# Gated linear attention beside a mixture of experts: exponentials one step later, and two waits among GpSimd's transfers

## What is computed

```python
xn = _layernorm(x, axis=-1)
x = x + _L0_attn_ref(xn, ...) + _L0_ffn_ref(xn, ...)

# attention, with gc the running sum of the log gates inside a chunk
A = jnp.einsum('bhntd,bhnsd->bhnts', q, k)
A = A * jnp.where(mask, jnp.exp(jnp.where(mask, dec, 0.0)), 0.0)   # dec = gc[t] - gc[s]
o_intra = jnp.einsum('bhnts,bhnsd->bhntd', A, v)
...
on = o * jax.lax.rsqrt(jnp.mean(o * o, axis=-1, keepdims=True) + EPS) * gnorm_w
o = on * (g * jax.nn.sigmoid(g))
return o @ Wo

# experts
for e in range(NUM_EXPERTS):
    h = jax.nn.gelu(x_flat @ w1[e] + b1[e], approximate=False)
    y = h @ w2[e] + b2[e]
    sel = expert_idx == e
    out = out + jnp.where(sel, expert_w, 0.0)[:, None] * y
```

## Time and profile before

| | us |
|---|---|
| median of 3 runs | 411.32 |
| lowest, highest | 410.52, 411.75 |
| the profiled execution | 410.52 |
| its span, first to last instruction | 408.6 |
| TensorE busy | 386.7 (95%) |
| VectorE busy | 326.3 (80%) |
| ScalarE busy | 304.5 (75%) |
| GpSimd busy | 276.6 (68%) |

### The profile page before, as it was taken

One profiled execution on the slowest core, in us unless ns is written; L12 is line 12 of the kernel. 1 busy time (PEld: TensorE's weight loads), 2 busy tenths in 40 slices (PEclk: granted clock), 3 DMA queues, 4 the chain that ended last, 5 costly groups with the idle time before them and its releaser, 6 DMA issues.

```text
span 408.6 us, 13495 instructions
## 1 busy us (share of the span) xinstructions
PE 386.7 (95%) x3650; PEld 337.1 (83%) x3651; DVE 326.3 (80%) x868; ACT 304.5 (75%) x947; POOL 276.6 (68%) x237
## 2 busy tenths in 40 slices
PE   7988899999999999999999999899999999999990
PEld 6656788877788888888888878799999999999990
DVE  5989898999988898889888888667687687687750
ACT  4889998787887978797888887466666676666660
POOL 6012534268888888888888833178888888888884
PEclk9999999999999999999999999999999999999996
DMA  8846586464555445474655340145545555455530
GB/s 237 230 158 193 177 288 245 120 186 129 170 179 162 128 127 168 143 200 140 186 155 154 115 137 14 44 63 69 69 68 65 66 69 67 63 67 71 64 32 0
DMA packets 59096, 51.29 MB, mean 126 GB/s; under 512 B 7200, under 2 KB 51392, under 8 KB 59072
## 3 DMA queue, kind: packets, MB, share of 16 engines
q1 hardware_dynamic: 45936, 42.07, 36.0%
q0 software_dynamic: 12272, 8.54, 15.1%
q10 hardware_dynamic: 864, 0.40, 0.4%
HBM read 33.14 MB, written 18.30 MB: 126 GB/s over the span
## 4 chain that ended last, share of the span: by engine, by line
PE 80%; DVE 6%; ACT 4%; DMA 3%; issue 3%; POOL 2%; SPq 1%; ACTq 0%; DVEq 0%; POOLq 0%
PE psA L912 16%; PE psVG L900 16%; PE psVG L721 9%; PE psO L756 8%; PE psA L737 7%; PE psT L790 6%; PE psQK L709 6%; PE psT L782 4%; PE psKS L747 3%; PE psO L770 3%; ACT E L1080 2%; SPq L343 1%; DMA x_all<-in_L_attn_x_dram 1%; DMA gcB<-decay_rows 1%; PE psQK L891 1%
## 5 line engine op out<-in xcount | busy, mean ns | idle before, releaser
L579 POOL DMA_INDIRECT out_dram<-yw,sidx x71 | 115.0, 1619 | 29.1 <-issue 11.6
L538 POOL TENSOR_TENSOR rms<-msn,neg_half 128x8 f32<-128x8 f32 x32 | 53.3, 1665 | 48.4 <-DVE msn L1412 44.7
L1080 ACT ACTIVATE E<-gcB,ngc 128x128 f32<-128x128 f32 x256 | 78.5, 397 | 0.4 <-DMA gcB<-decay_rows 0.4
L544 POOL DMA_INDIRECT sorted_rows<-x_all,pos_i x64 | 65.2, 1019 | 14.4 <-issue 10.5
L531 POOL TENSOR_SCALAR_AFFINE_SELECT E<-E 128x1024 f32<-128x1024 f32 x32 | 35.7, 1115 | 33.5 <-ACT E L1080 33.2
L756 PEld LDWEIGHTS psO<-v_sb,pr 128*64 128x64 f32 x1024 | 39.8, 137 | 12.0 <-issue 4.1
L756 PE MATMUL psO<-v_sb,pr 128*64 128x64 f32 x1024 | 44.5, 225 | 2.7 <-DVE pr L1440 2.5
L1089 ACT ACTIVATE sq<-psO 128x512 f32<-128x512 f32 x32 | 19.1, 597 | 33.4 <-PE psO L756 33.4
L1440 DVE TENSOR_TENSOR pr<-psA,E 128x512 f32<-128x512 f32 x64 | 41.0, 682 | 0.2
L912 PE MATMUL psA<-xT_all,v_sb 128*128 x288 | 38.3, 276 | 0.5 <-issue 0.4
L900 PE MATMUL psVG<-xgT,gcB 128*128 128x128 f32 x288 | 38.6, 277 | 0.0
(11 more groups left out here) (197 smaller groups left out, 928.5 us busy)
## 6 DMA issues: line engine op xcount, KB each, us to landing
gcB<-decay_rows SPq DMA_DIRECT2D x32, 512.0 KB
sorted_rows<-blank SPq DMA_DIRECT2D x12, 396.0 KB, 5.5
xg<-sorted_rows SPq DMA_DIRECT2D x71, 66.0 KB
x_all<-in_L_attn_x_dram SPq DMA_DIRECT2D x16, 256.0 KB, 5.3
out_dram<-res SPq DMA_DIRECT2D x32, 128.0 KB
eqB<-decay_exp_rows SPq DMA_DIRECT2D x32, 64.0 KB
w1b<-in_L_ffn_w_dram SPq DMA_DIRECT2D x8, 256.0 KB
xT_all<-in_L_ffn_w_dram SPq DMA_DIRECT2D x32, 64.0 KB
```

The costliest lines, as they stand in the source:

```text
L538: nc.gpsimd.tensor_tensor(rms[:], msn[:], neg_half[:, 0:2 * H], ALU.pow).then_inc(rms_ready, 1)
L544: nc.gpsimd.indirect_dma_start(out=sorted_dram, out_offset=bass.IndirectOffsetOnAxis(ap=pos_i[:, t:t + 1], axis=0), in_=x_all[:, t, :], in ...
L579: nc.gpsimd.indirect_dma_start(out=out_rows, out_offset=bass.IndirectOffsetOnAxis(ap=sidx[j][:], axis=0), in_=yw[j][:], in_offset=None, bo ...
L1080: last = nc.scalar.activation(E[j][:, k, h * P:(h + 1) * P], gcB[j][:, k * H + h, :], ACT.Exp, bias=ngcf[:, bass.ds((s * 2 + k) * H + h, 1)])
```

## The change

Two engines are rewritten. On ScalarE `exp_dec` moves from the step ahead (`turn(i, j, 1, 2)`, after the copy of oT) into the step itself, right behind x_hi and ahead of the square; the single call for sequence 2 ahead of the loop goes away. On GpSimd the mask of a sequence moves from the end of the step before to the front of its own step; the transfers are spread: t behind the mask and a wait for qk_ready (s + 2), t + 1 behind rms, t + 2 behind a wait for oT_ps_ready (s). The `t + 1 < TILES` test leaves out the last step, in which t + 1 and t + 2 do not exist. No instruction is added or removed apart from the waits.

```diff
@@ -546,24 +546,23 @@
 
             def step(s):
                 t = (s - PLACE_FROM) * 3
-                placing = s >= PLACE_FROM and t < TILES
-                if s == 0:
-                    mask_dec(0, 0)
+                if s < SEQS:
+                    mask_dec(*divmod(s, 2))
+                if s == PLACE_FROM:
+                    pool.wait_ge(dve_late, LATE)
+                    pool.wait_ge(sort_cleared, CLEARS * 16)
+                if s >= PLACE_FROM and t < TILES:
+                    pool.wait_ge(qk_ready, s + 2)
+                    place_rows(t)
                 if s >= 1:
                     if s >= 2:
                         pool.wait_ge(dve_on, s - 1)
                     rms_step(*divmod(s - 1, 2))
                 if s == 2:
                     finish_band()
-                if s == PLACE_FROM:
-                    pool.wait_ge(dve_late, LATE)
-                    pool.wait_ge(sort_cleared, CLEARS * 16)
-                if placing:
-                    place_rows(t)
+                if s >= PLACE_FROM and t + 1 < TILES:
                     place_rows(t + 1)
-                if s + 1 < SEQS:
-                    mask_dec(*divmod(s + 1, 2))
-                if placing:
+                    pool.wait_ge(oT_ps_ready, s)
                     place_rows(t + 2)
 
             for s in range(SEQS + 1):
@@ -1104,12 +1103,13 @@
             def step(i, j):
                 if inside(i, j, 1, SEQS):
                     split_hi(*turn(i, j, 1, 2))
+                if inside(i, j, 0, SEQS):
+                    exp_dec(i, j)
                 if inside(i, j, -1, SEQS):
                     square(*turn(i, j, -1, 2))
                 if inside(i, j, -2, SEQS):
                     copy_oT(*turn(i, j, -2, 2))
                 if inside(i, j, 1, SEQS):
-                    exp_dec(*turn(i, j, 1, 2))
                     copy_qk(*turn(i, j, 1, 2))
                     tanh(*turn(i, j, 1, 2))
                     copy_v(*turn(i, j, 1, 2))
@@ -1171,7 +1171,6 @@
             decay_keys(1)
             tanh(1, 0)
             copy_v(1, 0)
-            exp_dec(1, 0)
             step(1, 0)
             step(1, 1)
             soft_exps()
```

## The result

| | before | changed |
|---|---|---|
| median, us | 410.92 (4 runs) | 427.22 (4 runs) |
| lowest, highest | 410.44, 411.75 | 425.62, 427.73 |
| the profiled execution | 410.52 | 427.74 |
| its span | 408.6 | 426.0 |

The changed kernel takes 1.0387 times as long (95% interval 1.0352 to 1.0423): slower by 16.3 us. The forecast was slower by 2.9 us, with a range up to 418.0. The sign and the loop were right; the size was wrong by a factor of more than five, and the time lies outside the range.

The account below looks back on a forecast made before the run. TensorE was taken to set the pace, at 7.05 us a steady step. Ring +3.1, step 2 -0.9 and seam +0.7 gave +2.9 us: 413.4 on the profiled execution, named as 414.2 for the median; range 409.0 to 418.0.

Parts of the forecast that it names:

- What bounds the kernel: Steady attention steps: TensorE sets the pace, busy 132.86 of 133 us; three other engines have about 1 us room a step.
- ScalarE at nothing: Exponentials moved into their own step on ScalarE replace its 0.96 us wait; cost put at nothing in steady steps.
- the cover: Margin of og on VectorE before TensorE starts the outputs: about 0.1 us; if gone, up to 0.2 us a step lost.
- x_lo, 0.7 us a step freed and worth nothing: VectorE's subtraction x_lo no longer runs beside GpSimd's mask: some 0.7 us a step freed, off the path, no gain.
- Step 2, 0.9 us gained: Step 2: x_lo no longer waits for ScalarE's exponentials, so the projections' 0.94 us delay goes: 0.9 us gained.
- The ring: GpSimd's loop from one step's transposes to the next through oT_ps_ready: 7.26 us a step, steps 8 to 28, 3.1 us lost.
- the first term: Gap on GpSimd from the end of a step's transposes (T) to transfer t+2: 0.16 to 0.32 us, taken as 0.25.
- the rival for a costlier case: VectorE stretches a ring transfer, or og comes late: ring 7.45 to 7.6 us, +7 to +10, near 419.5; chance 0.10.
- the faster case: Rival: the ring closes in less than TensorE's step, 7.0 us, and disturbed steps heal: -2.6 us, 408.7; chance 0.24.
- qk_ready "is hidden": GpSimd's wait ahead of transfer t: semaphore comes at about T + 2.1, the mask ends at T + 2.35, so no cost.
- Step 7 at nothing: No cost was named for step 7; the ring was charged only for steps 8 to 28.
- The seam, 0.7 us: Passage to the expert part: step 31's exponentials delay step 30's square, then kd and the state product: 0.7 us lost.

Follow-up runs that it names:

- the two versions at 7.05: Kernel before with ScalarE's half alone, 409.35 us (ratio 0.9950); changed kernel without both waits, order kept, 409.52 us (ratio 0.9961).
- the first experiment: Changed kernel without the wait for oT_ps_ready ahead of transfer t+2, order kept: 425.36 us (expected about 410.5).

## Why the prediction was wrong in size

- **What bounds the kernel**: right. TensorE's full row meant that a new loop between engines shows at once when it is longer than 7.05 us.
- **ScalarE at nothing**: right for a steady step (7.05 in the kernel with this half alone). There og ended 0.67 us ahead of the outputs, where I had put the cover at 0.1. The outputs in the changed kernel do wait for og by 0.2 to 0.3 us, but the ring is longer, and it costs nothing.
- **x_lo, 0.7 us a step freed and worth nothing**: nothing speaks against it. It takes 0.42 in the changed kernel and in the two versions at 7.05, whose steady distance is that of before; but GpSimd is full there too, so what the freed time would be worth without that is not shown.
- **Step 2, 0.9 us gained**: 1.3 measured (7.04 against 8.30 us).
- **The ring**: its path, its order and eight of nine legs were right. The step that failed is the first term, "T to the start of transfer t+2 ... Between 0.16 and 0.32; I take 0.25". It was 0.82. In 21 steps that is 21 x 0.57 = 12.0 of the 13.4 us by which the forecast fell short. The bound came from GpSimd instructions that follow one another without an open wait, and from rms, which itself carries its wait. Neither has the form of the new code, where the waiting instruction is the increment and the transfer comes behind it. The text said that "No row shows a transfer that waits for TensorE", and yet put a narrow range on it; a transfer that waits for something else was there, at 266.18, with 0.89. Even the rival for a costlier case added at most 0.4 us a step, for another reason, a busy port; that cannot be the 0.82, since x_lo ended at 151.85 in the changed kernel and the transfer started 0.66 later. The warning of the Trainium skill, "SBUF — State Buffer", section "SBUF: two separate sides", that I gave for this rival is for VectorE operations in a two-port mode, and no run shows x_lo in one. Whether it is a part of the 0.28 is open: in the kernel with the increment ahead of the wait for oT_ps_ready, x_lo ended at 152.59 and the transfer started at 152.71. A slip besides: the low values that the text names add up to 7.15, not 7.09, and the faster case's own 408.7 lies outside the range of 409.0 to 418.0.
- **qk_ready "is hidden"**: right for the changed kernel in steps 8 to 28, with the row of the kernel without it (7.83). But the ring over it, 7.66, was not worked out, and without it my expectation for the first experiment missed.
- **Step 7 at nothing**: wrong, 1.3 us. It is the first step with the wait for qk_ready, rms stands behind it, and the mask is not late yet; the prediction began its ring one step later. The wait is 1.05 of it, as the kernel without it shows.
- **The seam, 0.7 us**: 0.54 in step 31 (6.50 against 5.96), in the way that was forecast, the state product waiting 0.49 us for kd; 0.4 from step 28 to the end.

Together: the 21 steps took 15.7 us more where 3.1 was forecast (12.6, of which 12.0 are the first term), step 7 adds 1.3, step 2 takes 0.4 off and the seam 0.3. That is 13.2 of the 13.4 us by which the forecast fell short.

## What to carry to other kernels

Before a wait is put into a queue, follow what stands behind it until the loop comes back to the semaphore, for every wait that is added and from the first step that has it; where two loops close, removing one shows only the other. Price the first leg of such a loop from a row in which the same kind of instruction stands behind an open wait, and where there is none, leave the range wide; look for it in the whole trace, whatever the wait is for, since a bracket can name another releaser than the one that came last. Here the same transfer started 0.82 or 0.28 us after the event, depending on whether a semaphore increment or the transfer itself carried the wait. Where a change has two halves, time each alone: one gave 0.5%, and the other hid it.

## What the runs showed of the hardware

- An indirect transfer issued by GpSimd starts 0.82 us after the event when another instruction ahead of it carries the open wait, 0.28 when it carries the wait itself, and 0.17 to 0.30 behind earlier work; a wait already met costs nothing (0.30), a memset starts 0.06 after the event, and a mask behind an increment that carries the wait 0.17. Two others behind such an increment had 0.89 (the first transfer into the output, behind a store's landing) and 1.10 (the first of all, at 83.55; why it is longer is not shown).
- A transfer that starts while the product on runs takes 1.50 us, against 0.96 and 0.98 for the two others of the step (the rows at 157.63, 152.51 and 154.76); I had put 1.0 to 1.2. It ends 0.91 us after on does (158.22), and 0.90 to 0.92 in the other steady steps, so it seems to be held until on is done. In the changed kernel msn, on 128x8 numbers, takes 0.17 us in one step and 1.77 in the next, in turn:

```profile
152.77 0.17 DVE L1411 SCALAR_TENSOR_TENSOR msn<-ms,vpe 128x8 f32<-128x8 f32 x1
...
160.35 0.96 POOL L544 DMA_INDIRECT sorted_rows<-x_all,pos_i  x1 [1.22 <-PE psT L781]
160.69 1.77 DVE L1411 SCALAR_TENSOR_TENSOR msn<-ms,vpe 128x8 f32<-128x8 f32 x1
...
161.32 1.11 POOL L531 TENSOR_SCALAR_AFFINE_SELECT E<-E 128x1024 f32<-128x1024 f32 x1
```

The long one ends at 162.46, with the mask (162.43). The Trainium skill, "SBUF — State Buffer", section "SBUF: two separate sides", has such an operation and one of GpSimd that reads SBUF exclude each other; the end together with the mask agrees. But the short msn ran while a transfer was under way (152.51 to 153.47), so the transfer did not hold the port for its whole length there; and what held the long one between 160.69 and the mask's start at 161.32 isn't shown.
